# A decoder layer on one core: the block-diagonal keys of pairs 1 to 7 copied by DMA instead of multiplied on GpSimd

## The reference

```python
def reference(x, ctx, Wq, Wk, Wv, Wo, ...):
    q, k, v = x @ Wq.T, x @ Wk.T, x @ Wv.T
    kvt = cumsum(k * v, axis=-2) * sqrt(256) / 128
    x = layernorm(x + (q * kvt) @ Wo.T)
    # cross attention, 32 query heads over 8 key heads of width 8; keys = values = ctx
    scores = einsum('bkgsd,bktd->bkgst', heads(x), heads(ctx)) / sqrt(8)
    x = layernorm(x + einsum('bkgst,bktd->bkgsd', softmax(scores), heads(ctx)))
    # feed-forward 256 -> 1024 -> 256 with block-quantised operands and a gelu
    x = layernorm(x + ffn(x))
    return x
```

## Time and profile before

| what | value |
|---|---|
| median of three runs | 292.05 us (291.25 to 292.17) |
| the profiled execution | 291.33 us, span 289.6 us |
| TensorE busy | 270.8 us (94%), 1640 matmuls |
| VectorE busy | 261.2 us (90%), 682 instructions |
| ScalarE busy | 220.2 us (76%), 378 instructions |
| GpSimd busy | 174.1 us (60%), 253 instructions |
| DMA | 12.68 MB, 44 GB/s over the span |

### The profile page before, as it was taken

One profiled execution on the slowest core, in us unless ns is written; L12 is line 12 of the kernel. 1 busy time (PEld: TensorE's weight loads), 2 busy tenths in 40 slices (PEclk: granted clock), 3 DMA queues, 4 the chain that ended last, 5 costly groups with the idle time before them and its releaser, 6 DMA issues.

```text
span 289.6 us, 5338 instructions
## 1 busy us (share of the span) xinstructions
PE 270.8 (94%) x1640; PEld 165.4 (57%) x1640; DVE 261.2 (90%) x682; ACT 220.2 (76%) x378; POOL 174.1 (60%) x253
## 2 busy tenths in 40 slices
PE   8999998999997998999989998999699989997799
PEld 3776755477554764676566756575346444543454
DVE  3799999996999999999999999999986997799982
ACT  5131866479999699979998889889998899875650
POOL 2746380698466787868786878667777353533321
PEclk9999999999999999999999999999869999999999
DMA  7931200002110020022002200210010000100111
GB/s 239 381 125 36 65 3 0 9 6 71 37 43 0 8 71 15 1 67 77 16 1 63 79 9 5 66 44 9 7 36 5 3 0 0 37 3 1 37 38 38
DMA packets 11053, 12.68 MB, mean 44 GB/s; under 512 B 3216, under 2 KB 8336, under 8 KB 10768
## 3 DMA queue, kind: packets, MB, share of 16 engines
q1 hardware_dynamic: 10592, 11.55, 12.5%
q10 hardware_dynamic: 432, 0.79, 0.7%
HBM read 9.84 MB, written 2.10 MB: 41 GB/s over the span
## 4 chain that ended last, share of the span: by engine, by line
PE 44%; DVE 37%; issue 8%; ACT 6%; POOL 3%; DMA 1%; DVEq 0%; POOLq 0%
DVE nm L1323 9%; PE bank L2122 6%; PE bank L2156 6%; PE bank L2169 5%; DVE st L1278 4%; PE bank L2007 3%; PE bank L2235 3%; PE bank L2210 3%; PE bank L2056 2%; PE bank L2082 2%; DVE gq L1424 2%; PE bank L2069 2%; PE bank L2208 2%; ACT g_sb L877 1%; PE bank L2177 1%
## 5 line engine op out<-in xcount | busy, mean ns | idle before, releaser
L1323 DVE TENSOR_REDUCE nm<-bank 128x4 f32<-128x512 f32 x128 | 83.8, 677 | 0.8 <-PE bank L2122 0.6
L857 ACT ACTIVATE p_sb<-bank 128x512 f32<-128x512 f32 x128 | 72.3, 599 | 12.1 <-PE bank L2156 11.6
L2122 PE MATMUL bank<-kbd,xT 96*128 96x512 f32 x128 | 56.0, 468 | 2.6 <-ACT xT L828 1.5
L2156 PE MATMUL bank<-xT,kbd 104*128 104x512 f32 x128 | 53.0, 444 | 5.3 <-DMA xT<-mT 3.2
L555 POOL TENSOR_TENSOR kbd<-k3r,diag_sb 96x512 fp32r<-96x512 f32 x32 | 33.2, 1052 | 12.9 <-PE bank L2156 12.9
L2156 PEld LDWEIGHTS bank<-xT,kbd 104*128 104x128 f32 x128 | 24.6, 193 | 18.6 <-ACT p_sb L857 6.4
L2122 PEld LDWEIGHTS bank<-kbd,xT 96*128 96x128 f32 x128 | 24.4, 193 | 17.9 <-DVE nm L1323 10.8
L2169 PE MATMUL bank<-p_sb,va_sb 128*32 128x512 f32 x256 | 33.3, 610 | 0.0
L509 POOL TENSOR_TENSOR rs<-ve,nhalf 128x2 f32<-128x2 f32 (+1 forms) x36 | 26.1, 725 | 4.6
L504 POOL TENSOR_SCALAR ve<-mv 128x2 f32<-128x2 f32 (+1 forms) x36 | 8.4, 234 | 33.5 <-DVE mv L1284 31.8
L2043 PE MATMUL bank<-wkv_r,xt_r 128*128 128x512 f32 x84 | 23.8, 405 | 0.7 <-DVE r_sb L1301 0.7
(11 more groups left out here) (133 smaller groups left out, 619.1 us busy)
## 6 DMA issues: line engine op xcount, KB each, us to landing
xt_sb<-in_xt SPq DMA_DIRECT2D x8, 256.0 KB, 2.9
x_sb<-in_x SPq DMA_DIRECT2D x8, 256.0 KB, 2.9
out_dram<-o_sb SPq DMA_DIRECT2D x7, 256.0 KB, 2.2
k_sb<-in_ctx SPq DMA_DIRECT2D x8, 192.0 KB, 3.0
x_all<-in_w SPq DMA_DIRECT2D x1, 1024.0 KB, 6.2
w_raw<-in_w SPq DMA_DIRECT2D x1, 1024.0 KB, 8.3
p_sb<-in_wkv ACTq DMA_DIRECT2D x2, 256.0 KB, 3.9
cv_sb<-in_ctxv SPq DMA_DIRECT2D x8, 64.0 KB, 2.0
```

Source lines behind the costliest of these rows:

```text
L857: sc.activation(p_sb[:, k, :], bankB[k % 2][:, :], ACT.Exp, scale=SCORE_SCALE).then_inc(s_ex, 1)
L1323: ve.tensor_reduce(nm[:, b, u, g, :], bankA[(2 + k + 11 * b) % 2][:, :].rearrange("p (k t) -> p k t", k=KU), AX.X, ALU.max, negate=True).t ...
L2122: mm(bankA[(2 + k + 11 * b) % 2][:, :], xT[0:MR, b, u, g, :], kbd[0:MR, b, u, :, :].rearrange("r k t -> r (k t)"), start=True, stop=True). ...
L2156: mm(bankB[k % 2][:, :], kbd[0:MR + 2 * KU, b, u, kk, :], xT[0:MR + 2 * KU, b, u, :, :].rearrange("r g s -> r (g s)"), start=True, stop=Tr ...
```

## The change

kbd becomes two buffers, used in turn by the pairs' parity. Pair 0 keeps the four products of GpSimd (now `first_keys`, with a semaphore of its own, s_kb0). For pairs 1 to 7 the products are gone from GpSimd's list, and SyncE issues four DMAs for each pair, SBUF to SBUF: the DMA of head k takes the rows k, k + 4, ... of k3r (24 rows, four runs of 512 bytes each, 48 KB) into the blocks of head k. The zeros between them are never written again: those of buffer 0 come from pair 0's products, those of buffer 1 from a new memset in GpSimd's setup. The fixed rows 96 to 103 of buffer 1 are copied from buffer 0 by one more DMA of SyncE, `second_diagonal` (64 KB). keys(p) waits for the rounded keys of the pair and for scores_b of pair p - 2; keys_rounded(p) now waits for the DMAs of pair p - 1 in place of its products. The lists of TensorE, VectorE and ScalarE are the same.

```diff
-        kbd = sb("kbd", [P, PB, U, KU, P], F32R)
+        kbd = [sb(f"kbd{n}", [P, PB, U, KU, P], F32R) for n in range(2)]
...
+            def second_diagonal():
+                sp.wait_ge(s_dgr, PB)
+                sp.dma_start(kbd[1][MR:MR + 2 * KU, :, :, :, :].rearrange("r b u k t -> r (b u k t)").bitcast(F32),
+                             kbd[0][MR:MR + 2 * KU, :, :, :, :].rearrange("r b u k t -> r (b u k t)").bitcast(F32)).then_inc(s_w["diag_rows"], 16)
+
+            def keys(p):
+                sp.wait_ge(s_k3r, 2 * p + 2)
+                if p == 1:
+                    sp.wait_ge(s_seta, 5)
+                else:
+                    sp.wait_ge(s_sbm, 16 * (p - 1))
+                for k in range(KU):
+                    sp.dma_start(kbd[p % 2][k:MR:KU, :, :, k, :].bitcast(F32), k3r[k:MR:KU, :, :, :].bitcast(F32)).then_inc(s_kbd, 16)
...
                 load_keys(1)
                 load_keys(2)
+                second_diagonal()
+                keys(1)
                 load_x(2)
                 load_xt(3)
                 load_values(2)
                 max_rows(1, 0)
                 max_rows(1, 1)
+                keys(2)
                 load_x(3)
                 load_keys(3)
                 spread_bias()
                 load_xt(4)
                 max_rows(2, 0)
+                keys(3)
                 load_values(3)
                 load_keys(4)
...
                 if on[1]:
                     load_x(p[1])
+                    keys(p[1])
                     load_values(p[1])
...
+                gp.memset(kbd[1][0:MR, :, :, :, :].rearrange("r b u k t -> r (b u k t)").bitcast(F32), 0.0).then_inc(s_seta, 1)
...
                 if later(p):
-                    pool.wait_ge(s_kbd, 4 * p)
+                    if p == 1:
+                        pool.wait_ge(s_kb0, 4)
+                    else:
+                        pool.wait_ge(s_kbd, 16 * KU * (p - 1))
...
-                keys(1, 0, 0)
-                keys(1, 0, 1)
-                keys(1, 1, 0)
                 var_eps(2, mv1, ve1, s_mv1, s_ve1)
                 rstd(2, ve1, rs1, s_ve1, s_rs1)
                 values(1)
-                keys(1, 1, 1)
...
                 if k == 0:
-                    pe.wait_ge(s_kbd, 4 * p + 2 * b + 2)
+                    if p == 0:
+                        pe.wait_ge(s_kb0, 2 * b + 2)
+                    else:
+                        pe.wait_ge(s_kbd, 16 * KU * p)
...
+                    if p == 1:
+                        pe.wait_ge(s_w["diag_rows"], 16)
...
```

More of the change, by code:

```diff
@@ L207, in ffn_bank @@
             return (bankP if b == 0 else bankA)[h]
-        s_w = {k: sem(f"loaded_{k}") for k in ("wkv0", "wkv1", "wq", "wo", "tri", "ident", "diag", "ln", "w1", "w2", "bias", "bias_rows")}
+        s_w = {k: sem(f"loaded_{k}") for k in ("wkv0", "wkv1", "wq", "wo", "tri", "ident", "diag", "ln", "w1", "w2", "bias", "bias_rows", "diag_rows")}
         s_x = sem("x_loaded")
@@ L247, in decoder_kernel @@
         s_k3r = sem("ctx_rounded")
+        s_kb0 = sem("first_keys_on_diagonal")
         s_kbd = sem("keys_on_diagonal")
@@ L472, in setup @@
                 gp.memset(nhalf[:, :], -0.5).then_inc(s_seta, 1)
+                gp.memset(kbd[1][0:MR, :, :, :, :].rearrange("r b u k t -> r (b u k t)").bitcast(F32), 0.0).then_inc(s_seta, 1)
                 gp.memset(ones_b[:, :], 1.0).then_inc(s_seta, 1)
-                pool.wait_ge(s_seta, 4)
+                pool.wait_ge(s_seta, 5)
                 gp.memset(va_heads[:, :, VH + DH:VH + DH + 1], 1.0).then_inc(s_seta, 1)
@@ L545, in keys_rounded, with first_keys @@
                 hold(pool)
-            def keys(p, b, u):
-                if not later(p) and b == 0 and u == 0:
+            def first_keys(b, u):
+                if b == 0 and u == 0:
                     pool.wait_ge(s_w["diag"], 16)
[L551 to L554, removed]
+                pool.wait_ge(s_k3r, 2)
                 gp.tensor_tensor(
-                    kbd[0:MR, b, u, :, :],
+                    kbd[0][0:MR, b, u, :, :],
                     k3r[:, b, u, :].bitcast(F32).unsqueeze(1).to_broadcast([MR, KU, P]),
-                    diag_sb[0:MR, :].unsqueeze(2).to_broadcast([MR, KU, P]), ALU.mult).then_inc(s_kbd, 1)
+                    diag_sb[0:MR, :].unsqueeze(2).to_broadcast([MR, KU, P]), ALU.mult).then_inc(s_kb0, 1)
             def x1_rows(p):
@@ L619, in head @@
                 split_xt_low(1)
-                keys(0, 0, 0)
-                keys(0, 0, 1)
+                first_keys(0, 0)
+                first_keys(0, 1)
                 var_eps(0, mv1, ve1, s_mv1, s_ve1, 0)
@@ L625, in head @@
                 split_xt_low(2)
-                keys(0, 1, 0)
+                first_keys(1, 0)
                 var_eps(0, mv1, ve1, s_mv1, s_ve1, 1)
                 rstd(0, ve1, rs1, s_ve1, s_rs1, 1)
-                keys(0, 1, 1)
+                first_keys(1, 1)
                 keys_rounded(1)
@@ L661, in head @@
                 weight3(0)
-                keys(2, 0, 0)
                 shift3(0)
-                keys(2, 0, 1)
                 split_xt_high(4)
-                keys(2, 1, 0)
-                keys(2, 1, 1)
                 keys_rounded(3)
@@ L698, in step @@
                     shift3(p[4])
-                if on[2]:
-                    keys(p[2], 0, 0)
-                    keys(p[2], 0, 1)
                 if on[5]:
@@ L707, in step @@
                     split_xt_low(p[0])
-                if on[2]:
-                    keys(p[2], 1, 0)
-                    keys(p[2], 1, 1)
                 if on[1]:
@@ L733, in tail @@
                 split_x1_high(7, 1)
-                keys(7, 0, 0)
                 var_eps(5, mv3, ve3, s_mv3, s_ve3)
@@ L738, in tail @@
                 shift3(5)
-                keys(7, 0, 1)
                 ffn_out(4)
                 residual3(4)
-                keys(7, 1, 0)
-                keys(7, 1, 1)
                 residual2(6)
@@ L1217, in diagonal_rows @@
                 for u in range(U):
-                    last = ve.tensor_copy(kbd[MR:P, b, u, :, :],
+                    last = ve.tensor_copy(kbd[0][MR:P, b, u, :, :],
                                           diag_sb[MR:P, :].unsqueeze(2).to_broadcast([P - MR, KU, P]))
@@ L2122, in scores_a @@
                 mm(bankA[(2 + k + 11 * b) % 2][:, :], xT[0:MR, b, u, g, :],
-                   kbd[0:MR, b, u, :, :].rearrange("r k t -> r (k t)"), start=True, stop=True).then_inc(s_sa, 1)
+                   kbd[p % 2][0:MR, b, u, :, :].rearrange("r k t -> r (k t)"), start=True, stop=True).then_inc(s_sa, 1)
             def maxT(p, b):
@@ L2153, in scores_b @@
                         pe.wait_ge(s_dgr, b + 1)
+                    if p == 1:
+                        pe.wait_ge(s_w["diag_rows"], 16)
                 if b or k >= 2 or later(p):
                     pe.wait_ge(s_ex, 16 * p + 8 * b + k - 1)
-                mm(bankB[k % 2][:, :], kbd[0:MR + 2 * KU, b, u, kk, :],
+                mm(bankB[k % 2][:, :], kbd[p % 2][0:MR + 2 * KU, b, u, kk, :],
                    xT[0:MR + 2 * KU, b, u, :, :].rearrange("r g s -> r (g s)"),
```

## The result

The kernel after takes 306.0 us (median of 4 runs, 305.48 to 306.42), the kernel before in the same session 291.69 us (4 runs): a ratio of 1.048 [1.044, 1.052], 14.3 us slower. The forecast was 304.0, slower, inside 298.5 to 309. The profiled execution is the slowest of the four, 306.42 us, so against the 291.33 of the profile before there are 15.1 us to account for. Of all runs used here one is left out of its ratio as a slow one, the 309.47 us of e3, over 1.5% above the fastest run of its kernel.

What follows compares the result with a forecast made beforehand. The chain runs through TensorE and VectorE; GpSimd, busy for 174.1 us, has only 3% of it. Terms 10.7 + 2.3 + 0.5 - 0.8 = 12.7 us on the profiled 291.33 gave 304.0 us, range 298.5 to 309.

Steps and rivals of the forecast that it cites:

- Steps 1 to 5: In the head, second_diagonal's wait and the issues behind it hold load_xt(3), GpSimd's splits and x1T(1,0,0): 12.0 us of delay.
- Steps 6 and 7: Between x1T(1,0,0) and kv_proj(3): 1.3 us of TensorE's waits given back, 2.3 us lost to a 1.2 GHz clock.
- Step 8: SyncE's later queue: keys(2) pushes the bias rows back by 2.4 us, and TensorE waits 0.5 us for them.
- The gain in step 8 of the pipeline: VectorE's L1416, on the chain there, loses its collision with a GpSimd product: 0.8 us saved, taken once.
- A: Faster: the held loads in the head are covered and only GpSimd's relief is left; 286 us, chance 0.04.
- B: Head stall comes, but more is given back by clock, landing and all collisions; 297 us, chance 0.14.
- step 1: In the head, VectorE ends diagonal_rows(1) at 42.1 us, 2.14 us sooner than 44.21.
- the collisions of the steps: In steps 5 to 8, VectorE's L1416 falls on GpSimd products; all of them paying would give 2.4 us more.
- D: No change: the head stall is just paid back, 12 us from work off the chain; chance 0.02.
- C: Head stall comes and later max_rows(p, 0) slip, 1 us each, by slow issues or late keys; 310 us, chance 0.12.

Runs made afterwards that it cites:

- e3: Kernel after with 54 matmuls on zeros ahead of x1T(1,0,0), to fill TensorE's stall: ratio 1.048 to the kernel before.
- e1: Kernel before with only SyncE's wait for both diagonal_rows added ahead of load_x(2): 299.86 us, ratio 1.027.
- e2: Kernel after with second_diagonal moved behind load_x(2) and load_xt(3), all copies kept: 290.92 us, ratio 0.9967.
- e4: Kernel after with spread_bias moved from behind keys(2) to ahead of load_values(2): 304.45 us, ratio 1.042.
- e6: Kernel after with second_diagonal behind load_xt(3) and spread_bias ahead of load_values(2): 289.98 us, ratio 0.9933.
- e8: Kernel after with keys(1) moved behind load_xt(3), second_diagonal and its wait still ahead: 303.05 us, ratio 1.038.
- e9: Kernel after with 40 matmuls on zeros ahead of x1T(1,0,0): 306.28 us, ratio 1.049.
- e10: As e6, with keys(p) in the steps also moved behind max_rows(p, 0) of the pair ahead: 289.72 us, ratio 0.9928.
- e5: Kernel before with GpSimd's products of pairs 1 to 7 cut to 4 of 128 columns, no copies: 289.58 us, ratio 0.9928.
- e7: As e6, with four spare DMAs of half the bytes ahead of the keys of each of pairs 4 to 7: 303.5 us, ratio 1.040.

## Why the prediction was right, and where it was off

**The step that carries it** is the wait in second_diagonal, and it held: x1T 12.9 us late against a forecast of 12.0. e1 shows it alone, e2 shows that without it there is no loss at all. Steps 1 to 5 in numbers:

| term | forecast | after |
|---|---|---|
| diagonal_rows(1) ends | 42.1 | 41.76 |
| second_diagonal, issue | 0.45 | 0.81 |
| keys(1), four issues | 4 x 0.6 | 3.35, 0.84 each |
| load_xt(3) issues | 45.4 | 46.67 |
| landing | 3.4 | 2.9 |
| x1T(1, 0, 0) | 51.9 | 52.81 |

x1T came 0.9 us later than forecast. The mis-sized term is the issue: 0.36 us too little for second_diagonal and 0.95 for keys(1), 1.3 us on the path to load_xt(3), and 0.3 in load_x(2) and the gaps between issues; against it stand 0.3 at the end of diagonal_rows and 0.5 at the landing. I took it from issues that move few or long rows (0.43 for a plain load, 0.63 for the bias rows); a copy with 24 partitions of four separate runs takes SyncE 0.84 us, and one of eight long rows inside SBUF 0.81. The landing was shorter than the row I chose and close to the other bound, 2.8.

**Steps 6 and 7.** Forecast: 1.3 us given back, 2.3 for the clock, so 13.0 - 12.0 = 1.0 more between x1T and kv_proj(3). The kernel after has 0.1 more. That the delay at kv_proj(3) is 13.0 as forecast is luck: 0.9 too little up to x1T and 0.9 too much behind it cancel. By e3's profile, whose clock stayed up, the same work takes 4.14 us in place of 6.20 before: 2.1 given back, and 2.1 lost to the clock. Both sizes are from one execution of e3, whose other runs do not bear out a gain.

By the Trainium skill ("TensorE: Matmul & The Clock Gate", Terms), the loss is put at half the length of a slow stretch, so an estimate by that page for the 13.7 us is 6.8. The trace disagrees, with 2.1: for 9 of those 13.7 us TensorE had nothing to run.

**Step 8.** Forecast 0.5 us of wait for the bias rows; TensorE waited 0.85 and the delay grew by 0.9. The issues pushed back were 0.83 each here too. e4, which has no such wait, gives some 1.0 back at the same mean clock.

**The gain in step 8 of the pipeline** (0.8 us at L1416) came to 0.2. The delay goes from 203.31 - 188.20 = 15.1 us at one max_rows to 217.29 - 202.41 = 14.9 at the next. Part of this is a wrong reading of a mean. The seven narrow instructions aren't alike: in the kernel before four of them, one in each of steps 5 to 8, take 0.96 us and three take 0.17 or 0.18, so the 0.625 us of the earlier trace rows isn't a loss of 0.45 each. After, all seven take 0.17 or 0.18, which saves 4 x 0.79 us. But the groups of VectorE before and after, narrow hq,

```profile
L1424 DVE TENSOR_TENSOR hq<-z,sc 128x512 bf16<-128x512 bf16 x7 | 5.4, 766 | 0.2
```

```profile
L1419 DVE TENSOR_SCALAR sc<-am 128x16 bf16<-128x16 f32 x7 | 1.2, 175 | 0.2
L1427 DVE TENSOR_TENSOR hq<-z,sc 128x512 bf16<-128x512 bf16 x7 | 6.8, 973 | 0.2
```

show 1.4 us of the 3.2 given back a few instructions later. With GpSimd still, hq takes 0.42 us (at 85.36 in the kernel after). In the four steps it overlaps GpSimd's L626 (L605 before) and ends 0.3 us behind that instruction in both kernels: at 133.78 against 133.50 before, at 132.10 against 131.81 in e6. L626 starts when ScalarE's y_sb is there, so it comes no sooner for a faster VectorE. The rest of the saving in e6's first step is VectorE's wait of 0.36 us for TensorE. The Trainium skill ("SBUF — State Buffer", SBUF: two separate sides) has such a pair, a VectorE operation with two SBUF inputs against a GpSimd operation that reads SBUF, as one that blocks. That fits e6's rows: 1.39 us with L626 beside it.

**Not forecast at all**: the dip of the clock at 105.2 us, 1.2 us. It is in the profiles of the kernel after, e8 and e9, and not in those of e1, e2, e3, e4, e6 and e10. The change isn't needed for it. The profile of e5, a kernel without copies and without a stall, has one 9.9 us ahead of the same max_rows (99.00), where the kernel after has it 9.3 ahead (114.48):

```profile
89.10:92.50 3.40, 3.40 (x16) 2.63 (x13) 3.40 (x9) 2.06 (x5) 2.69 (x5) 0.50 0.00 0
```

The kernel before runs in two kinds as well. Of its 13 runs in the session of e1, seven have a mean granted clock of 0.988 and took 291.13 to 291.55 us, six have 0.982 and took 292.11 to 293.64. The profiled execution before has 0.988. So this 1.2 us belongs to the two executions that are compared, and not surely to the change. What sets it off is open.

**The sum**: 12.9 + 0.1 + 0.9 + 1.2 = 15.1 for the profiled execution, against the forecast 10.7 + 2.3 + 0.5 - 0.8 = 12.7. The 0.2 us of step 8 are lost again behind it; the clock there is at 0.50 for 10.2 us from 221.2, where the kernel before has 6.8 us, but no run shows what that costs.

**The rivals.** A (held loads covered) is excluded by the stall. B's relief is real, about 2 us (e5, e6), but it is the 2.1 us that the forecast already had in its step 1; the collisions of the steps gave the 0.2 us above, and in e5 and e6 TensorE's lead doesn't grow at the product of 68.83. D, no change, is excluded by the same stall. C didn't happen: from max_rows to max_rows the steps keep their 29.6 us (114.48, 144.03, 173.67). The slack was thin: keys(p) and load_values(p) end at 128.01 and max_rows issues at 128.48, 0.5 us where 1 was forecast, and e7 shows what lies behind it.

## What to carry to other kernels

Before an instruction with a wait goes into an in-order queue, write down when that wait ends and list everything behind it; here one wait held a load that three engines then stood for, while the copy behind the wait could be issued after the load at no cost. Moving the copy with its wait three places down turned 14.3 us of loss into a gain of 0.6 us, and with the bias rows moved as well 1.7. Count DMA issues by their shape when they stand on a queue's path (0.84 us for a strided one, twice a plain load). Relief for an engine off the chain paid here at the one collision that stood on the chain; in the steps the saved time went into a wait for TensorE and into the next collision. And before a mean of a group is priced, look whether its members are alike.

## What the runs showed of the hardware

- The issue time of a DMA on SyncE depends on its shape: 0.46 us for a plain load of 128 rows, 0.63 for max_rows, 0.72 (e2) and 0.81 (kernel after) for 64 KB in eight long rows inside SBUF, 0.84 for 48 KB in 96 runs of 512 bytes. Half the bytes in the same shape took 0.83 (e7, at 107.75), so it isn't the bytes. It isn't the shape alone either: load_keys took 0.32 us at 26.96 in the kernel after, and 1.35 at 83.62 in e3, behind the copies of keys(2) and load_x(3).
- In the kernel after, the granted clock stayed at 0.50 for 4.6 us after TensorE had work again, and in a wait of 3.8 us in a step (e7) it fell to 0.50 for 6.8 us. A step of e7 lost 4.4 us to 3.3 us of issues.
- Executions of one kernel differ by short falls of the granted clock: the kernel before took 291.13 to 291.55 us at a mean clock of 0.988 and 292.11 to 293.64 at 0.982. Such a fall, 3.4 us long, cost 1.2 us in the kernel after and 1.1 in e5.
- A VectorE operation with two SBUF inputs took 0.42 us alone and 1.39 us when it started with a GpSimd operation of 1.16 us; it ended 0.3 us behind it.
- 54 products of zeros in the stall kept the clock at 1.00 in the profiled run of e3 (the profile has 52 of them), and 40 (39 in the profile of e9), which ended 4.2 us ahead of the next work, didn't.
